# An attention and feed-forward block on Trainium2: the second h load waits for the projection's weights, the last weight casts are issued one unit earlier, and Tanh's table is read in the first stage

## The reference

```python
xn  = layernorm(x)                       # no scale, no shift
qkv = xn @ W_attn + b_attn               # 16 heads of 64
att = (q @ k.T) / 8 / temperature + slope[h] * (pos_k - pos_q), causal
y   = softmax(att) @ v
h   = silu(xn @ wg.T / 127) * (xn @ wu.T / 127)    # 3072 hidden, integer weights
out = x + (y @ W_proj + b_proj) + h @ wd.T / 127
```

## Time and profile before

| | us |
|---|---|
| median of 3 runs (lowest to highest) | 970.81 (969.37 to 971.08) |
| profiled execution, its own time | 971.7 |
| span of the slowest core in it (core 2) | 970.1 |
| spans of the cores | 963.1 to 970.1 |
| PE busy (share of the span) | 897.8 (93%) |
| DVE, ACT, POOL busy | 501.0, 481.2, 284.9 |

### The profile page before, as it was taken

The page is one execution under the profiler, slowest core; times in us unless marked ns, Lnnn a source line. Parts: engine busy times, 40 slices in busy tenths (PEclk is TensorE's granted clock), DMA queues, the critical chain, the costliest instruction groups (busy, mean ns, idle before and its releaser), DMA issues.

```text
span 970.1 us, 18969 instructions; the slowest of 8 cores (963.1 to 970.1 us)
## 1 busy us (share of the span) xinstructions
PE 897.8 (93%) x6163; PEld 407.3 (42%) x6274; DVE 501.0 (52%) x1113; ACT 481.2 (50%) x583; POOL 284.9 (29%) x305
## 2 busy tenths in 40 slices
PE   1899899999999999999999999999989699999998
PEld 1445334444444444444444444344434244444443
DVE  3642377677777777777777777777310011110111
ACT  1445477676777667777767767766426000000000
POOL 2010133433333333233333233344462042412200
PEclk9999999999999999999999999999999799999999
DMA  8726189999999999999999999899689967352211
GB/s 180 194 83 109 20 164 224 222 212 188 160 222 208 208 214 191 190 212 193 199 213 210 184 190 189 192 206 211 132 181 244 199 181 258 129 185 77 87 44 44
DMA packets 334388, 168.56 MB, mean 174 GB/s; under 512 B 305491, under 2 KB 317780, under 8 KB 333140
## 3 DMA queue, kind: packets, MB, share of 16 engines
q1 hardware_dynamic: 325360, 133.21, 68.1%
q0 software_dynamic: 5328, 22.02, 11.6%
q10 hardware_dynamic: 3604, 12.11, 3.4%
HBM read 84.46 MB, written 20.97 MB: 109 GB/s over the span
## 4 chain that ended last, share of the span: by engine, by line
PE 74%; DMA 8%; issue 6%; DVE 5%; SPq 3%; ACT 2%; POOL 0%; DVEq 0%; ACTq 0%; another core or an unknown queue 0%; POOLq 0%
PE ps_gu L733 27%; PE ps_dn L852 15%; PE ps_m L713 9%; PE ps_s L797 7%; PE ps_dn L846 6%; PE ps_y L810 6%; PE ps_s L766 4%; DMA wdres<-wd_r 4%; SPq L304 3%; DMA xstage<-xin 2%; DVE sc L541 2%; ACT pr L657 1%; DVE hst L484 1%; DMA bv_s<-battn_v 1%; PE ps_y L713 1%
## 5 line engine op out<-in xcount | busy, mean ns | idle before, releaser
L657 ACT ACTIVATE pr<-sc,cm 128x2048 bf16<-128x2048 f32 (+15 forms) x256 | 290.6, 1196 | 60.1 <-DVE cm L541 60.0
L541 DVE CUSTOM_DVE_ANT_0 sc<-ps_s,ramp 128x1024 f32<-128x1024 f32 (+7 forms) x256 | 243.8, 988 | 73.0 <-PE ps_s L797 62.7
L733 PE MATMUL ps_gu<-xnT,wubuf 128*128 128x512 bf16 x738 | 198.0, 382 | 15.8 <-DVE hst L484 14.3
L733 PE MATMUL ps_gu<-xnT,wgbuf 128*128 128x512 bf16 x730 | 195.9, 380 | 8.1 <-ACT gh_s L611 6.1
L852 PE MATMUL ps_dn<-wdres,hb 128*128 128x512 bf16 x752 | 169.3, 382 | 9.9 <-DMA wdres<-wd_r 9.0
L399 POOL TENSOR_SCALAR th_s<-th_s 128x512 f32<-128x512 f32 x96 | 59.2, 617 | 275.1 <-ACT th_s L609 275.0
L582 DVE SCALAR_TENSOR_TENSOR outsb<-ps_dn,xres 128x512 f32<-128x512 f32 x32 | 20.7, 687 | 213.3 <-PE ps_dn L852 149.6
L541 DVE CUSTOM_DVE_ANT_0 sc<-ps_s,ramp,cm 128x1024 f32<-128x1024 f32 (+7 forms) x128 | 99.9, 815 | 56.3 <-PE ps_s L797 55.4
L405 POOL TENSOR_TENSOR gs_s<-th_s,gh_s 128x512 bf16<-128x512 f32 x96 | 111.2, 1158 | 27.5 <-POOL th_s L399 25.4
L852 PEld LDWEIGHTS ps_dn<-wdres,hb 128*128 128x128 bf16 x768 | 75.5, 98 | 101.5 <-issue 12.5
L713 PE MATMUL ps_m<-xnT,wqk_b 128*128 128x512 bf16 x466 | 112.2, 380 | 0.6 <-issue 0.2
(11 more groups left out here) (56 smaller groups left out, 454.6 us busy)
## 6 DMA issues: line engine op xcount, KB each, us to landing
h_sc<-hst SPq DMA_DIRECT2D x96, 128.0 KB, 3.2
stg_i<-wg_r SPq DMA_DIRECT2D x20, 512.0 KB, 5.1
stg_i<-wu_r SPq DMA_DIRECT2D x20, 512.0 KB, 5.2
hb<-h_sc SPq DMA_DIRECT2D x3, 3072.0 KB, 15.5
xstage<-xin SPq DMA_DIRECT2D x16, 512.0 KB, 7.5
xres<-xin POOLq DMA_DIRECT2D x16, 512.0 KB, 5.6
out<-outsb ACTq DMA_DIRECT2D x15, 512.0 KB, 2.8
stg_f<-wqk_r SPq DMA_DIRECT2D x12, 512.0 KB, 5.5
```

Source lines behind the costliest of these rows:

```text
L541: e.tensor_tensor_reduce(scores(n, g + (2 if b == 2 else 0), c0, w), ps_s[:, g * 1024:g * 1024 + w], ramp[:, T - wide + c0:T - wide + c0 + ...
L657: e.activation(pr[n % 3][:, b0 * 128:(b0 + blocks) * 128], scores(n, r, 0, blocks * 128), AF.Exp, bias=cm[:, at:at + 1], scale=-1.0).then_ ...
L733: mm = e.matmul(ps_gu[:, up * 512:up * 512 + 512], w[:, w0:w0 + 128], xnT[:, dc * T + tb * 512:dc * T + tb * 512 + 512], start=(dc == 0), ...
```

## The change

Three edits. SP waits for `l_wp` as well before it loads `hb1`. The six parts of `late_weights` follow silus 89 to 94 instead of 90 to 95. ACT computes a Tanh of one column, whose result nobody reads, in step 16 of the first stage.

```diff
+        warm = sb(st, "warm", [128, 1], F32)
...
             for tb in range(1, NTB):
                 e.wait_ge(sem[f"s_h{tb}"], 16 * HCN)
                 if tb == 1:
                     e.wait_ge(sem["p_u"], NF)
+                    e.wait_ge(sem["l_wp"], 16)
...
             for f in range(NF_ATT + 1, NF):
                 gate_and_loads(f)
-                if NF_ATT + 2 <= f < NF_ATT + 2 + HCP // 2:
-                    late_weights(f - NF_ATT - 2)
+                if f < NF_ATT + 1 + HCP // 2:
+                    late_weights(f - NF_ATT - 1)
...
                     e.activation(sd[b][:, :], mv[b][:, 1:2], AF.Sqrt, bias=eps_s[:, :]).then_inc(sem["a_sd"], 1)
+                if i == NT:
+                    e.activation(warm[:, :], eps_s[:, :], AF.Tanh)
                 if i == 4:
```

## The result

The changed kernel takes 965.0 us (median of 6 runs) against 970.78 for the one before (6 runs). Two of the six were slow executions (999.65 and 1097.13 us, one die at a lower clock); every ratio here is of the undisturbed runs alone. It is 0.9935, with a 95% interval of 0.9921 to 0.9950, so it is 6.3 us faster (4.9 to 7.7). A second series of 5 runs gave 965.13 and 0.9937 (0.9925 to 0.9949). The forecast was 961.3, a gain of 9.5, in a range of 956.5 to 967.

A forecast was written before the change was run, and what follows sets the result against it. PE's queue was taken as the bound, through the projections' start plus 183.0 us. Core 6's span 969.2 less 7.7, less Tanh's 0.9, made 960.6, plus 1.6 was 962.2, against the median 961.3; range 956.5 to 967.

The forecast's parts named there:

- rival 1: Last stage: hst stores get in the way more, core 6 starts h kinds 3.5 to 5 us later; 965 to 966.5, chance 0.12.
- Bound by the projections' start plus 183.0: Last stage: each core's span is its start of the projections plus 183.0 us; 1.6 more gives the profiled time.
- The projections' start, 778.5 less Tanh's 0.9: Core 6, forecast as last: h kinds from 737.01 plus 41.45 us put the projections at 778.5; Tanh's table takes off 0.9.
- The load of hb1: Before the projections: moved behind the weights, it lets them land up to 9.6 us sooner and itself takes 15.5 us.
- Casts a unit sooner, 3.45 us on the landing: Late weight casts on q0: issued a unit earlier, they land 3.45 us sooner, between 0 and 3.45.
- The price at the stores, taken as 0, bounded by 3.5 us: hst stores beside earlier casts, DVE waiting at f = 92 and 94: 0 assumed, bounds +3.5 and -5.35 us.
- What I said of stores 88 and 89: hst stores near the first casts: 89 already shared its whole time with casts, 88 goes out before they flow.
- PE becomes the bound: Before the projections: PE's h kinds, 41.45 us, end after the weights on core 6, by 5.4 us.
- Tanh's table, 0.9, at most 1.28: Before gate group 1: loading the table in the first stage gains 0.9 us, between 0 and 1.28.
- drain of the page's rule: First stage table switch: a drain of about 1380 ns would make PE wait 0.9 us and leave a gain of about 0.
- 2.2 us for a slow clock: Last stage: 96 matmuls behind the wait for weights take 22.96 us, against 20.7 at full clock.

The follow-up runs named there:

- cast_only: The kernel before with only the late-weight casts moved a unit sooner, hb1's load left beside them; 972.5 us, ratio 1.0022.
- casts_later: The changed kernel with the casts a unit later than in the kernel before, four hst buffers; 960.16 us, ratio 0.9890.
- hb_only: The kernel before with only hb1's load made to wait for the projection's weights; 963.22 us, ratio 0.9925.
- hb_tanh: The changed kernel with the casts back in their old place, hb1's wait and the early Tanh table kept; 962.5 us, ratio 0.9918.
- eight_hst: The changed kernel with four more hst buffers for groups 92 to 95, so no tail group waits for a store; 961.1 us, ratio 0.9896.
- eight_hst_casts_back: The changed kernel with four more hst buffers and the casts back in their old place; 961.86 us, ratio 0.9916.
- tanh_only: The kernel before with only Tanh's table loaded early, in the first stage; 968.27 us, ratio 0.9979.

## Why the prediction was right, and where it was off

The direction and the range held; the gain was 6.3 us where 9.5 were forecast. The median of 965.0 lies just above the 959 to 964.5 that had the chance 0.60, at the lower end of rival 1. Step by step:

- **Bound by the projections' start plus 183.0.** Right: 961.7 - 778.75 = 183.0 on core 4, and 182.9 to 183.0 on all eight. It isn't a constant of every variant. Before, it was 183.0 behind waits of 1.0 to 2.9 us for `wpj_b`; on the late cores of cast_only it is 185.5 to 185.8 behind waits of 3.9 to 4.2 (971.1 - 785.35 on core 4), on those of casts_later 184.2 to 185.6 behind 3.5 to 4.1, and in hb_only and hb_tanh the stretch at a clock of 0.81 adds to it.
- **The projections' start, 778.5 less Tanh's 0.9.** Close for a wrong reason. The forecast took core 6's late exit from the first stage, with its last keys at 104.12 us; core 4 had them at 102.45. Behind the last keys the forecast was 778.5 - 0.9 - 104.12 = 673.5 us, and the late cores have 675.2 to 676.3. So 2.3 us in the mean were lost that the earlier exit of this one execution gave back.
- **The load of hb1.** Right, in kind and size: 10.1 us (hb_only) for 9.6. `hb1` landed in 15.1 us, the row at 801 us had said 15.5. The first residual add began at 773.74 on core 4, in time.
- **Casts a unit sooner, 3.45 us on the landing.** Wrong. I took the time before the first cast as free. ACT's `hb0` pieces had filled the engines already, and an earlier cast pushed other work back. The worth of this step is 0 with the change's other edits (eight_hst against eight_hst_casts_back, casts_later) and 1.3 us of landing without them (cast_only), and the casts could have begun two units later at no cost.
- **The price at the stores, taken as 0, bounded by 3.5 us.** This is the step that took the gain away, and the bound was too narrow. From the Tanh of group 88 to the first h kind the late cores need 39.7 to 40.5 us, and 33.2 to 36.2 before: 5.5 us more in the mean. What I said of stores 88 and 89 was right: 1.7 and 12.8 us, for 3.0 and 12.7 before. I hadn't looked at the two behind them. The stores stand in one queue, and each is slowed by casts and `hb0` together: store 90 takes 16.3 us instead of 12.8 and store 91 19.8 instead of 14.2 (core 4, against core 2 before), a delay that grows from store to store and is paid at f = 94. It is the mechanism of rival 1, whose 965 to 966.5 holds the measured time. As an edit of its own the earlier cast costs 2.1 us (1.1 to 3.2); inside the change it costs 858.8 - 855.5 = 3.3 us without the first stage, 1.6 by the ratios, whose intervals overlap.
- **PE becomes the bound.** Right: no wait for weights on any core.
- **Tanh's table, 0.9, at most 1.28.** Right where the clock had stayed up: 1.0 us is left at group 88. On the cores whose clock had fallen behind the longer wait it is 2.5 to 2.7, above my bound, as I had no term for the clock there; 2.0 measured (1.1 to 2.9). Of the drain of the page's rule (the Trainium skill, ScalarE: Activation LUTs, What ACT_TABLE_LOAD costs) the trace shows nothing: the keys' copy ends at 88.44, the load starts at 88.45, and the small activation follows it at 89.75. The measurement decides, and no 0.9 us are lost in the first stage: PE shows no wait at this place.

The sum by the runs: -7.3 (hb_only), -2.0 (tanh_only), +2.1 (cast_only) make -7.2, and -6.3 were measured (4.9 to 7.7), so that the three add up within the noise. Two slips in the working, 787.0 for the row's 787.13 and 2.2 us for a slow clock that cost 2.1 once the last matmul's 0.16 is taken off, don't move the forecast.

## What to carry to other kernels

When transfers are moved to start earlier, first look whether the DMA engines are idle in the time they are moved into. If another queue fills them, the landing stays where it is and only the order changes, and what pays is the small store that now shares with one queue more. Variants that started the same casts up to two units apart had the weights within 1 us of each other, and of these the one with the fewest transfers beside the stores had the lowest median, by less than the noise against eight_hst.

In a stage whose DMA engines are full, taking one wait away shows the next: stores, then the projection's weights, then `hb1`, then the residuals, all within 2 to 5 us. My guess, which wasn't tried, is that to get well below 960 us here one would have to load less before the projections, not in another order.

## What the runs showed of the hardware

- In one execution of the kernel before, the 8 matmuls behind a wait of 2.60 us ran at a low clock on core 1 (3.51 us for the 8) and at the full one on core 2 (1.89 us). A wait of 3.46 us left the clock up on core 1 of hb_only (1.89 us for 8, granted clock 1.00), one of 4.06 us on core 4 of hb_tanh didn't (3.57 us, 0.50). The length of a wait alone doesn't tell.
- The clock also fell without a wait: in hb_only and hb_tanh it was 0.81 for some 14 us on all four cores of one die at once, with PE busy in all of it.
- Three DMA queues that had work at the same time got through the same number of packets (41, 39 and 42 in 2.2 us), whatever their size, and so through very different shares of the time (49.1%, 46.4% and 7.0%).
- The late and the early cores change places from execution to execution, with mostly 3 to 5 us between them out of the first stage. A comparison of single cores by number would have been misleading.
